# Moving every fourth product of scan states with C from VectorE to GpSimd in a fused Mamba, FFN and linear-attention kernel

## The reference, cut to what matters

```
dt = softplus(dt_low @ w_dt + b_dt) * (DT_MAX - DT_MIN) + DT_MIN
step:  barA = exp(dt * A)                      # b, d, n
       h = barA * h + inp_term[:, None, :]
       y = einsum('bdn,bn->bd', h, C) + Dp * u
x = x + scan(norm(x)); x = x + ffn(norm(x)); x = x + attention(norm(x)); x = x + ffn(norm(x))
```

## Time and profile before

| | before |
|---|---|
| median of 3 runs | 2455.58 us (2453.37 to 2623.25) |
| the profiled execution's own time | 2458.8 us |
| its span in the profile | 2457.1 us |
| granted TensorE clock, mean | 0.935 of full speed |
| PE, DVE, ACT, POOL busy | 85%, 86%, 73%, 38% of the span |
| C matmuls of two neighbouring batches | 1138.64 and about 1279.6 us: a batch takes 140.9 us |

### The profile page before, as it was taken

How to read it: one execution, slowest core, us unless ns; L and a number is a source line. 1 busy time by engine, 2 the same in 40 slices (tenths; PEclk the granted TensorE clock), 3 DMA queues, 4 the chain that set the end, 5 groups by cost and what they waited for, 6 DMA issues and landing times.

```text
span 2457.1 us, 40388 instructions
## 1 busy us (share of the span) xinstructions
PE 2094.8 (85%) x12780; PEld 1312.6 (53%) x12844; DVE 2122.1 (86%) x4102; ACT 1802.1 (73%) x3549; POOL 943.2 (38%) x1656
## 2 busy tenths in 40 slices
PE   2438799898989989898989989898998989899986
PEld 1104556464655646465564646465564646556563
DVE  6788798989989898989989898998989899897743
ACT  4477779696878869687887969787786968766441
POOL 3003344344434443443444344343443444344442
PEclk8568899999999999999999999999999999999997
DMA  3342322313232232323123131322223132321000
GB/s 86 81 125 64 86 70 62 85 48 99 54 91 54 66 82 59 88 54 97 54 77 82 47 101 46 102 54 76 69 65 82 51 97 55 82 60 30 5 6 9
DMA packets 104432, 165.95 MB, mean 68 GB/s; under 512 B 15442, under 2 KB 34078, under 8 KB 104222
## 3 DMA queue, kind: packets, MB, share of 16 engines
q1 hardware_dynamic: 104222, 163.37, 24.7%
HBM read 146.55 MB, written 16.78 MB: 66 GB/s over the span
## 4 chain that ended last, share of the span: by engine, by line
PE 52%; ACT 19%; DVE 18%; issue 8%; POOL 4%; DMA 0%; ACTq 0%; POOLq 0%; SPq 0%; DVEq 0%
PE bank L953 12%; PE bank L968 11%; PE bank L950 4%; DVE scan_bufs L1254 4%; PE acc_y L918 4%; PE bank L989 3%; DVE scan_bufs L1264 3%; PE bank L962 2%; PE bank L1006 2%; ACT masked_scores L715 2%; ACT scan_bufs L647 2%; POOL f_h L566 2%; ACT scan_bufs L654 2%; ACT f_hqT L715 2%; PE bank L1034 2%
## 5 line engine op out<-in xcount | busy, mean ns | idle before, releaser
L1254 DVE TENSOR_TENSOR_SCAN scan_bufs<-scan_bufs,inp_bank 128x512 f32<-128x512 f32 x512 | 614.8, 1201 | 18.9 <-ACT scan_bufs L654 18.9
L953 PE MATMUL bank<-w_gu,f_xqT 128*128 128x512 f32 x1024 | 478.4, 609 | 6.7 <-ACT f_xqT L715 3.8
L647 ACT ACTIVATE scan_bufs<-scan_bufs,a_rows 128x512 f32<-128x512 f32 x512 | 367.8, 718 | 15.0 <-DMA scan_bufs<-dt_copy 14.8
L968 PE MATMUL bank<-w_dn,f_hqT 128*128 128x256 f32 x1536 | 363.9, 387 | 3.2 <-ACT f_hqT L715 3.2
L1264 DVE TENSOR_TENSOR scan_bufs<-scan_bufs,c_bank 128x512 f32<-128x512 f32 x512 | 344.1, 672 | 2.7 <-PE c_bank L906 0.6
L968 PEld LDWEIGHTS bank<-w_dn,f_hqT 128*128 128x128 f32 x1536 | 289.3, 193 | 78.9 <-issue 40.7
L654 ACT ACTIVATE scan_bufs<-scan_bufs 128x512 f32<-128x512 f32 x512 | 321.6, 628 | 0.0
L953 PEld LDWEIGHTS bank<-w_gu,f_xqT 128*128 128x128 f32 x1024 | 196.8, 199 | 222.9 <-issue 205.9
L566 POOL TENSOR_TENSOR f_h<-f_h,f_h_inv 128x704 f32<-128x704 f32 x128 | 178.5, 1394 | 307.5 <-DVE f_h_inv L1152 307.4
L566 POOL TENSOR_TENSOR f_h<-f_h,f_h_scale 128x704 f32<-128x704 f32 x128 | 179.4, 1401 | 299.4 <-DVE f_h L1114 299.4
L918 PE MATMUL acc_y<-scan_bufs,sel_y 128*32 128x512 f32 x1024 | 162.3, 711 | 104.2 <-DVE scan_bufs L1264 104.2
(11 more groups left out here) (202 smaller groups left out, 4234.0 us busy)
## 6 DMA issues: line engine op xcount, KB each, us to landing
scan_bufs<-dt_copy SPq DMA_DIRECT2D x512, 256.0 KB, 3.9
xp<-L_attn_a_x SPq DMA_DIRECT2D x16, 512.0 KB, 4.2
dt_copy<-dt SPq DMA_DIRECT2D x32, 256.0 KB, 4.0
out<-x SPq DMA_DIRECT2D x64, 128.0 KB, 3.5
w_attn<-L_attn_b_W_attn SPq DMA_DIRECT2D x1, 768.0 KB
scan_bufs<-L_ffn_w_gate SPq DMA_DIRECT2D x1, 704.0 KB
scan_bufs<-L_ffn_w_up SPq DMA_DIRECT2D x1, 704.0 KB
masked_scores<-L_ffn_w_down SPq DMA_DIRECT2D x1, 704.0 KB
```

The lines of the kernel that those rows point to most:

```text
L647: nc.scalar.activation(half, half, ACT.Exp, scale=a_rows[:, c, at:at + 1]).then_inc(root_ready, 1)
L953: last = nc.tensor.matmul(to[:, :], f.xqT[:, k, :], w_gu[:, k, g, lo:hi], start=(k == 0), stop=(k == DH - 1))
L968: last = nc.tensor.matmul(to[:, 0:D], f.hqT[:, k, :], w_dn[:, k, :], start=(k == 0), stop=(k == FK - 1))
L1254: nc.vector.tensor_tensor_scan(half, half, inp[:, :], 0.0, ALU.mult, ALU.add)\
```

## The change

Products m = 3, 7, ..., 31 of each batch (8 of 32) go to GpSimd. It can't read PSUM, so ScalarE copies C from `c_rep` into a new SBUF tile `c_copy` once a batch, and GpSimd takes the product from there, in place in the slot. TensorE's sum waits for both counts of products. The next C matmul waits for DVE's products of the batch before and for the copy, and the next copy waits for GpSimd's last product of the batch before. DVE's first product now waits for the copy. All numbers in `TIMES` are new, and `LAST_AT["R2"]` starts at 95.7 and no longer at 93.7.

```diff
+POOL_EVERY = 4
...
-LAST_AT = {"R1": (66, 3), "R2": (93.7, 3.5)}
+LAST_AT = {"R1": (66, 3), "R2": (95.7, 3.5)}
...
     "pe": {
-        ("P", "B"): 13.687, ("P", "C"): 31.332, ("P", "dt0"): 12.333, ("P", "dt1"): 14.797, ("P", "G"): 29.653,
-        ("G", "sum"): 3.634, ("Y", "turn"): -0.688, ("R1", "turn_x"): 5.363, ("R1", "up0"): 6.264,
...
-        ("R1", "a_qkv"): 14.993, ("R1", "a_s0"): 17.022, ("R1", "a_s1"): 17.757, ("R1", "a_sum"): 19.482,
-        ("R1", "a_flip"): 20.316, ("R1", "a_turn_y"): 21.66, ("R1", "a_proj"): 24.101, ("R2", "turn_x"): 2.725,
+        ("P", "B"): 10.135, ("P", "C"): 31.118, ("P", "dt0"): 14.022, ("P", "dt1"): 14.072, ("P", "G"): 29.475,
+        ("G", "sum"): 3.339, ("Y", "turn"): -1.394, ("R1", "turn_x"): 5.775, ("R1", "up0"): 6.176,
...
+        ("R1", "a_qkv"): 14.79, ("R1", "a_s0"): 17.329, ("R1", "a_s1"): 17.56, ("R1", "a_sum"): 19.091,
+        ("R1", "a_flip"): 22.043, ("R1", "a_turn_y"): 25.034, ("R1", "a_proj"): 26.428, ("R2", "turn_x"): 3.249,
...
     "act": {
-        ("M", "square"): -1.484, ("R1", "a_root"): 15.896, ("R1", "a_qkv"): 16.001, ("R1", "a_v"): 16.311,
+        ("P", "C"): 32.446,
...
     "dve": {
-        ("P", "inp"): 31.678, ("M", "scan"): -0.165, ("M", "read"): 0.445, ("S", "skip"): -0.121,
+        ("P", "inp"): 31.33, ("M", "scan"): -0.65, ("M", "read"): 0.648, ("S", "skip"): -1.169,
...
     "pool": {
+        ("R1", "a_proj"): 30.626, ("R1", "below2"): 30.959, ("M", "read"): 0.535,
...
+def on_pool(m):
+
+    return m % POOL_EVERY == POOL_EVERY - 1
+
+
+def reads_upto(b, m, pool):
+
+    return sum(on_pool(i) == pool for i in range(HALVES)) * b + sum(on_pool(i) == pool for i in range(m + 1))
...
+            def read_state(b, m):
+
+                n, h = divmod(m, DH)
+                half = bar[slot_of(b, n)[0]][:, h, :]
+                if on_pool(m):
+                    pool.wait_ge(c_copied, upto(b, 1, 0))
+                    pool.wait_ge(scans_done, upto(b, HALVES, m))
+                    pool.tensor_tensor(half, half, c_copy[:, :], ALU.mult).then_inc(pool_read, 1)
...
+            def copy_c(b):
+
+                act.wait_ge(c_ready, upto(b, 1, 0))
+                if not first(b):
+                    act.wait_ge(pool_read, reads_upto(b - 1, HALVES - 1, True))
+                nc.scalar.activation(c_copy[:, :], c_rep[:, :], ACT.Copy).then_inc(c_copied, 1)
...
                 if not first(b):
-                    pe.wait_ge(read_out, upto(b - 1, HALVES, HALVES - 1))
+                    pe.wait_ge(read_out, reads_upto(b - 1, HALVES - 1, False))
+                    pe.wait_ge(c_copied, upto(b - 1, 1, 0))
...
-                pe.wait_ge(read_out, upto(b, NS // DH, g, 2 * DH))
+                pe.wait_ge(read_out, reads_upto(b, 2 * DH * (g + 1) - 1, False))
+                pe.wait_ge(pool_read, reads_upto(b, 2 * DH * (g + 1) - 1, True))
...
                 if m == 0:
-                    dve.wait_ge(c_ready, upto(b, 1, 0))
-                dve.wait_ge(scans_done, upto(b, HALVES, m))
-                nc.vector.tensor_tensor(half, half, c_rep[:, :], ALU.mult).then_inc(read_out, 1)
+                    dve.wait_ge(c_copied, upto(b, 1, 0))
+                if not on_pool(m):
+                    dve.wait_ge(scans_done, upto(b, HALVES, m))
+                    nc.vector.tensor_tensor(half, half, c_rep[:, :], ALU.mult).then_inc(read_out, 1)
```

More of the change, by code:

```diff
@@ L35 @@
 HALVES = NS * DH
+POOL_EVERY = 4
 N_SETUP_POOL = 34
 PARTS_AT = {"P": (0, 0, 1), "M": (32, 1, 32), "D": (32, 2, 16), "G": (32, 4, 8), "S": (48.95, 16, 2), "Y": (65.0, 1, 2), "R1": (66, 3, 4), "R2": (95.7, 7, 4)}
-LAST_AT = {"R1": (66, 3), "R2": (93.7, 3.5)}
+LAST_AT = {"R1": (66, 3), "R2": (95.7, 3.5)}
 TIMES = {
     "sp": {
-        ("P", "load"): -0.497, ("P", "keep0"): 20.63, ("P", "keep1"): 27.582, ("D", "spread"): -9.609,
-        ("R2", "down"): 18.594,
+        ("P", "load"): -2.517, ("P", "keep0"): 19.192, ("P", "keep1"): 30.328, ("D", "spread"): -12.018,
+        ("R2", "down"): 18.757,
     },
     "pe": {
[7 rows of a table removed]
[7 rows of a table added]
     },
     "act": {
[13 rows of a table removed]
[14 rows of a table added]
     },
     "dve": {
[14 rows of a table removed]
[14 rows of a table added]
     },
     "pool": {
[5 rows of a table removed]
[5 rows of a table added]
     },
@@ L249, in build @@
         sp_exp, sp_inv = (p_xT[:, 0, :], du[:, 0, :]), (p_xT[:, 1, :], du[:, 1, :])
-        b_rep = sb("b_rep", [P, T])
+        b_rep, c_copy = sb("b_rep", [P, T]), sb("c_copy", [P, T])
         scan_bufs = sb("scan_bufs", [P, SLOTS, DH, T])
@@ L344, in build @@
         root_ready, a_root_ready = sem("root_ready"), sem("a_root_ready")
-        read_out, summed, c_ready = sem("read_out"), sem("summed"), sem("c_ready")
+        read_out, pool_read, summed, c_ready = sem("read_out"), sem("pool_read"), sem("summed"), sem("c_ready")
+        c_copied = sem("c_copied")
         skip_ready = sem("skip_ready")
@@ L604, in _ @@
             for b, q, part, t, step in steps_of("pool"):
-                if part == "P":
+                if part == "M":
+                    read_state(b, t)
+                elif part == "P":
                     part_p(b, q, step)
@@ L808, in _ @@
                     (decay if step == "decay" else square)(b, t)
+                elif step == "C":
+                    copy_c(b)
                 elif part == "P":
```

## The result

The changed kernel takes 2499.07 us (median of 4 runs, 2497.72 to 2501.18), the kernel before took 2454.47 in the runs beside it. One slow run of the kernel before, 2623.25, is not in the ratio. The ratio is 1.0189, with a 95% interval of 1.0173 to 1.0205: 1.9% slower, where 1.4% faster was forecast; that is at the edge of the 2% that the chances were parted by, and above the range. The profiled execution's span is 2499.3 us, 42.2 more than before, at a clock of 0.928 (0.935 before).

What follows compares the result with a forecast made beforehand. DVE bounds a batch's first stretch, PE the second, neither the third. Gains and losses of 1.5 - 0.4 + 1.2 = 2.3 us a batch, 37 us over 16, take 2458.8 to 2422, as median 2420 us (-1.4%); range 2370 to 2472.

Steps and rivals of the forecast that it cites:

- The new beats: Attention steps get more other work between them, so PE idles less: 1.2 us a batch gained, bounds 4.8 either way.
- The drain's new place: The new place of R2 in the drain behind the last scan was costed at nothing.
- Products off DVE: Eight products fewer on DVE; only 2.5 in the DVE-bound stretch count, 0.59 us each: 1.5 us a batch gained.
- the lock: POOL's product and two-input DVE instructions shut each other out: 0.4 us a batch lost, bounds 0 and 1.5.
- Product on POOL: One product of 512 elements takes 1.27 us on POOL, lower end 1.06; POOL doesn't become the bound.
- The exclusion: Two-input DVE instructions wait while POOL's product runs: 0.4 us a batch lost, bounds 0 and 1.5.
- The sign that was given: DVE's two-input instructions longer by more than 25 us in all would prove the forecast wrong, through the lock.
- The sum's wait: PE's 4.22 us wait before the first group's sum: latency 0.2 to 0.4 us longer, costed at nothing.
- The copy: ACT's copy of C, 0.59 us once a batch, is hidden and costs nothing; bounds 0 and 0.6 us a batch.
- POOL late at the sums: Slower rival: products queue behind POOL's FFN scalings and PE waits at sums, 4.3 us a batch net, 2528 us; chance 0.12.

Runs made afterwards that it cites:

- e15: The kernel before, old beats, no copy, with products m = 3, 7, ..., 31 left out altogether: 2442.8 us, ratio 0.9949.
- e17: The kernel before with the new beats, no copy, and products m = 3, 7, ..., 31 left out altogether: 2520.4 us, ratio 1.026.
- e6: The changed kernel with the old beats, its products on POOL later in the queue (1.02, not 0.445), the copy at 32.35: 2497.5 us, ratio 1.0174.
- e5: The changed kernel with the attention's last steps and `LAST_AT["R2"]` back at the old numbers: 2613.6 us, ratio 1.0653.
- e16: The kernel before, old beats, with eight late products (m = 14, 16, ..., 28) left out altogether: 2457.6 us, ratio 1.0009.
- e8: The changed kernel with the old beats, products m = 1, 5, ..., 29 on POOL at beat 1.5, the copy at 32.35: 2501.7 us, ratio 1.0196.
- e10: As e8, but with each product on POOL replaced by two memsets: 2472.4 us, ratio 1.0075.
- e3: The changed kernel, new beats, with each product on POOL replaced by two memsets: 2493.3 us, ratio 1.0155.
- e12: The kernel before, old beats, with only the copy of C and its waits added, no product moved: 2454.9 us, ratio 1.0008.

## Why the prediction was wrong, step by step

- *The new beats, +1.2 us a batch.* **This step failed**, in sign and size, where the eight products are left out: the order costs 78 us (e15, e17), of which 18 are the drain (348 against 330) and 60 the batches and the start, 3.7 a batch. Where they are on POOL, it costs 2 us against e6: the drain is 14 longer (348 against 334) and a batch 0.5 shorter (142.9 against 143.4), less than the 1.2 that was forecast. So the drain is lost either way, and the batch's loss is shown only without the products. The bounds of ±4.8 held it; the value was chosen from one pair of numbers, the attention's 2.95 beats, as though more distance could only help. The attention's own waits grew instead (`masked_scores` from 13.5 to 20.0 us in seven batches), and steps that I had not looked at now wait: `low`, `f_x`.
- *The drain's new place, nothing.* Failed as well: 17.1 us. The place was not the cause (e5); by the table and the waits the R2 beats within it were. This could have been worked out from the diff: gap 3.5, `up0` and `up1` against `turn_h`.
- *Products off DVE, 1.5 us a batch.* The mechanism was right (late ones 0, e16), the size was 0.85 (e15).
- *What a product on POOL holds up, nothing but the lock.* **This term was missing.** At the old beats the move makes a batch longer and not shorter, by 2.3 us in e6 (143.4 for 141.1) and 2.9 in e8 (144.0), and with memsets in the products' place (e10) it is still 1.0 longer (142.1). The forecast had POOL's queue only as a rival of 0.12, and for the sums alone.
- *Product on POOL, 1.27 us.* 1.30 measured. DVE is busy for 2087.6, forecast some 2040: with the products gone altogether it is 2055.3 (e15), and the longer roundings, below, make up 28 of the other 32.
- *The exclusion, 0.4 us a batch.* Under-sized for products 1, 5, ... at the old beats: 1.8 a batch (e10), over its upper bound of 1.5. I counted the 32 roundings and left out `f_x_scale` and `kv`, which account for 22.1 of the 42.3 us. At the new beats it is 5.8 us in all (e3). The sign that was given, over 25 us more on two-input instructions, came up with 28 (553 - 411 and 494 - 419 ns, each 128 times; near 0 for the hidden vector), and it would have misled: e17 has 17 of them with no product on POOL (520 and 441 ns), and e3 with memsets has them too (520 and 440), presumably from POOL's own scalings at their new places. Only 11 are the products'.
- *The sum's wait, nothing.* It got shorter, by 2.6 us a batch in its longest wait. The latency did grow: from the end of scan 3 to the first sum 0.96 us passed before and 1.53 pass now (1162.13 to 1163.66), 0.57 longer where 0.2 to 0.4 was forecast. With the eight products on neither engine the waits for sums are 89.9 us at the old beats (e15) and 61.9 at the new ones (e17), so it is the order that shortens them, and it loses more elsewhere.
- *The copy, nothing.* Right (e12).
- *The rivals.* The slow one, POOL late at the sums, did not happen: those waits fell. At the old beats it is seen: in e6 PE stands 91.2 us for POOL's products. The kernel ended on the slow side by a mechanism that I had priced inside the forecast and not as a rival.

The account of the change, then: with the old beats the move costs 43 to 48 us (e6, e8), and with the new ones, which fit it, 45. The gain that these eight could bring at the old beats is 13.6. The parts don't add: the order costs 78 us with the products left out and, against e6, 2 with them moved. The changed kernel is 21 us faster than e17, which does less: 12.4 of them lie in the seven batches, where PE stands equally long in both (100.4 and 100.3 us) and its own work takes 12.5 less, at a clock of 0.96 for 0.95. What keeps the clock up, and which beats cost the batch its 1.8 us, stays open.

## What to carry to other kernels

Work taken from the busiest engine is worth what leaving it out altogether gives, and that can be measured first; here it was 0.6%, and only the first few products had it. When an order that is written by hand changes with it, compare for each wait of the critical engine which step stands behind it in the queue, at the ends of the program too: that one row cost more than the move could give. Move the few instructions that stand where the engine is the bound, at places where the receiving engine is idle and its own steps are not waited for.

## What the runs showed of the hardware

- A VectorE instruction of 16 elements, `f_x_scale`, one input in SBUF, was held for 1.07 us by a GpSimd product of 1.27 (0.17 to 1.24). It ended with the product, at 1214.28 and 1214.25: what it paid was the product's length, seven times its own.
- GpSimd memsets left two-input instructions alone (419 and 411 ns in e10, as before), but `f_x_scale` still took 219 ns on average, against 175 before.
- A product from PSUM was not held: 674 ns on average with POOL's products beside it, 672 before.
